# Dense layer 2 of a graph network kernel: rounding moved to GpSimd, another ScalarE order, three pairs of part buffers

## The reference, cut to what matters

```python
def _bn(h, g, b):
    mean = h.mean(0)
    var = h.var(0)
    return (h - mean) * jax.lax.rsqrt(var + EPS) * g + b
...
y = x + aggr
h = jnp.maximum(_bn(y @ W1 + b1, g1, be1), 0.0)
h = jnp.maximum(_bn(h @ W2 + b2, g2, be2), 0.0)
return y + h
```

## Time and profile before

| what | value |
|---|---|
| median of three runs | 2009.98 us |
| profiled execution, and its span | 2003.11 us, 2001.3 us |
| layer 2, from its first subtraction to its last | 626.1 to 925.7 us of the span |
| its blocks 20 to 97 | 688.1 to 925.7 us, 237.6 us |
| engines in that stretch | PE 234.2 us busy, DVE 221.0, ACT 211.4, POOL 0 |
| the 16 DMA engines from 700 to 790 us | busy share 0.98, 347 GB/s |

### The profile page before, as it was taken

How to read it: one execution, slowest core, us unless ns; L and a number is a source line. 1 busy time by engine, 2 the same in 40 slices (tenths; PEclk the granted TensorE clock), 3 DMA queues, 4 the chain that set the end, 5 groups by cost and what they waited for, 6 DMA issues and landing times. The chain is left out here.

```text
span 2001.3 us, 27312 instructions
## 1 busy us (share of the span) xinstructions
PE 1774.9 (89%) x8655; PEld 1386.4 (69%) x8655; DVE 1624.2 (81%) x2365; ACT 1304.9 (65%) x1818; POOL 1088.0 (54%) x1200
## 2 busy tenths in 40 slices
PE   4687489999998999999999989965999999999994
PEld 3465378888886776766666666644788888888883
DVE  4678556766767999997999999994888888888884
ACT  1434246565656898887788888871666666666663
POOL 7556456676786400000555555566876576765553
PEclk8889899999999999999999999986999999999997
DMA  9999999999996899983699999974565532322110
GB/s 344 366 348 394 364 359 346 335 342 331 340 244 141 241 348 348 325 299 124 245 378 390 385 410 390 390 286 126 161 168 146 145 89 92 92 83 75 58 43 29
DMA packets 187567, 506.47 MB, mean 253 GB/s; under 512 B 26355, under 2 KB 79505, under 8 KB 187168
## 3 DMA queue, kind: packets, MB, share of 16 engines
q1 hardware_dynamic: 129888, 379.91, 51.9%
q0 software_dynamic: 47136, 73.62, 16.3%
q10 hardware_dynamic: 10400, 51.20, 6.7%
HBM read 323.94 MB, written 236.25 MB: 280 GB/s over the span
## 5 line engine op out<-in xcount | busy, mean ns | idle before, releaser
L607 POOL DMA_INDIRECT scratch_y<-sums,k_target x196 | 312.7, 1595 | 159.9 <-issue 79.9
L1041 ACT ACTIVATE d_o<-d_u,d_free 128x256 f32<-128x256 f32 x392 | 203.1, 589 | 64.0 <-POOL d_free L1078 64.0
L1015 PEld LDWEIGHTS d_pN<-k_ident,d_r 128*128 128x128 f32 x1568 | 192.0, 193 | 52.1 <-issue 46.4
L1010 PE MATMUL d_pN<-d_y,d_free 128*128 128x512 f32 x392 | 191.9, 612 | 33.6 <-DVE d_u L1104 30.1
L1015 PE MATMUL d_pN<-k_ident,d_r 128*128 128x128 f32 x1568 | 192.7, 276 | 4.9 <-ACT d_r L1030 4.9
L818 ACT ACTIVATE d_part_h<-pT 128x1024 fp32r<-128x1024 f32 x98 | 100.5, 1027 | 139.5 <-PE pT L785 125.1
L882 DVE TENSOR_TENSOR d_part_l<-pT,d_part_h 128x1024 fp32r<-128x1024 f32 x98 | 119.9, 1224 | 85.0 <-ACT d_part_h L818 85.0
L1075 POOL TENSOR_TENSOR d_free<-d_free,k_minus_half 128x8 f32<-128x8 f32 (+1 forms) x100 | 163.7, 1637 | 0.2
L1104 DVE SCALAR_TENSOR_TENSOR d_u<-d_pN,d_free,k_base 128x256 f32<-128x256 f32 x392 | 160.9, 472 | 0.0
L252 POOL DMA_INDIRECT k_ring<-in_x,k_src x100 | 120.9, 1209 | 68.7 <-PE pT L280 40.3
L61 PE MATMUL pU<-d_part_h,k_w_h 128*128 128x512 f32 x296 | 125.5, 424 | 27.2 <-DVE d_part_l L882 14.2
(11 more groups left out here) (227 smaller groups left out, 5209.7 us busy)
## 6 DMA issues: line engine op xcount, KB each, us to landing
scratch_h<-d_h SPq DMA_DIRECT2D x159, 512.0 KB, 5.9
out<-d_o SPq DMA_DIRECT2D x97, 520.0 KB, 6.0
k_ring<-scratch_y SPq DMA_DIRECT2D x98, 512.0 KB, 7.7
d_y<-scratch_y SPq DMA_DIRECT2D x98, 512.0 KB, 7.8
scratch_y<-in_x ACTq DMA_DIRECT2D x25, 2000.0 KB, 20.7
d_h<-scratch_h SPq DMA_DIRECT2D x81, 512.0 KB, 7.1
k_ring<-scratch_h SPq DMA_DIRECT2D x78, 512.0 KB, 5.2
attr<-in_attr_t SPq DMA_DIRECT2D x25, 512.0 KB, 15.1
```

Source lines behind the costliest of these rows:

```text
L607: pool.indirect_dma_start(out=A["y"], out_offset=bass.IndirectOffsetOnAxis(ap=K.target[:, t:t + 1], axis=0), in_=K.sums[:, t], in_offset=N ...
L1010: pe.matmul(pN[k % 4][:, 2 * two:2 * two + 2].rearrange("p j f -> p (j f)"), twice[:], y[:, k % 4, two * 2 * F:(two + 1) * 2 * F], start=T ...
L1015: last = pe.matmul(pN[k % 4][:, j, cc * P:(cc + 1) * P], r[:, k % 4, cc, j * P:(j + 1) * P], K.ident[:], start=False, stop=j % 2 == 1 and ...
L1041: last = act.activation(o[:, k % 4, j, 0:F], u[:, k % 3, j], ACT.Identity, bias=nb[:, n, j:j + 1], scale=rs[:, n, J + j:J + j + 1])
```

## The change

1. From block 20 of layer 2 on (`POOL_FROM`), GpSimd rounds every block: 78 copies of 128x1024 from r to the high part, 26 of which were ScalarE's and 52 VectorE's. Blocks 0 to 19 keep the old turn.
2. Layer 2 has three pairs of high and low parts. The third pair (`third_h`, `third_l`) lies in a piece of `sums` behind the held blocks, tiles 64 to 71. A rounding now waits for the product of block g-3 (`wait_part`), and at block 2 for the scatters that read these tiles.
3. In a turn ScalarE does `relu(g+2)` ahead of `out(g-2)`, not behind it.

```diff
+POOL_FROM = 20
...
     def hi_on_scalar(g):
-        return g % 3 == 0
+        return g % 3 == 0 and g < NB + POOL_FROM
+
+    def hi_on_pool(g):
+        return g >= NB + POOL_FROM
...
+    def parts_of(g):
+
+        at = (g - NB) % 3 if layer2(g) else g % 2
+        return (part_h[:, at], part_l[:, at]) if at < 2 else (third_h[:], third_l[:])
+
+    def wait_part(engine, g):
+
+        if g >= NB + 3:
+            engine.wait_ge(product, g - 2)
+        elif g == NB + 2:
+            for q in range(4):
+                engine.wait_ge(halved_in[q], 16 * (HELD_SUMS + 2))
+        else:
+            engine.wait_ge(product, g - 1)
...
+        for g in range(NB, 2 * NB):
+            if hi_on_pool(g):
+                pool.wait_ge(relu_done, g - NB + 1)
+                wait_part(pool, g)
+                pool.tensor_copy(parts_of(g)[0], r[:, g % 2]).then_inc(hi2_pool, 1)
...
             if hi_on_scalar(g):
                 act.wait_ge(relu_done, g - NB + 1)
-                act.wait_ge(product, g - 1)
-                act.activation(part_h[:, g % 2], r[:, g % 2], ACT.Copy).then_inc(hi2_scalar, 1)
+                wait_part(act, g)
+                act.activation(parts_of(g)[0], r[:, g % 2], ACT.Copy).then_inc(hi2_scalar, 1)
...
             if g + 1 < 2 * NB:
                 hi2(g + 1)
+            if g + 2 < 2 * NB:
+                relu(g + 2)
             if g >= NB + 2:
                 out(g - 2)
-            if g + 2 < 2 * NB:
-                relu(g + 2)
...
             if hi_on_scalar(g):
                 dve.wait_ge(hi2_scalar, on_scalar)
+            elif hi_on_pool(g):
+                dve.wait_ge(hi2_pool, on_pool)
             else:
                 dve.wait_ge(relu_done, g - NB + 1)
-                dve.wait_ge(product, g - 1)
-                dve.tensor_copy(part_h[:, g % 2], r[:, g % 2]).then_inc(hi2_vector, 1)
-                dve.wait_ge(hi2_vector, g + 1 - NB - on_scalar)
-            dve.tensor_tensor(out=part_l[:, g % 2], in0=r[:, g % 2], in1=part_h[:, g % 2].bitcast(F32),
-                              op=ALU.subtract).then_inc(lo_done, 1)
+                wait_part(dve, g)
+                dve.tensor_copy(parts_of(g)[0], r[:, g % 2]).then_inc(hi2_vector, 1)
+                dve.wait_ge(hi2_vector, g + 1 - NB - on_scalar - on_pool)
+            high, low = parts_of(g)
+            dve.tensor_tensor(out=low, in0=r[:, g % 2], in1=high.bitcast(F32), op=ALU.subtract).then_inc(lo_done, 1)
```

More of the change, by code:

```diff
@@ L650, in dense12 @@
     early = ET * 3 // 4
-    assert HELD_SUMS * J <= early
+    assert (HELD_SUMS + 2) * J <= early
     passes = [(1, k) for k in range(NB)] + [(2, (NB - HOLD + n) % NB) for n in range(NB)]
@@ L657, in dense12 @@
     part_h, part_l, h, held, r, _ = K.shared_second
+    third_h, third_l = K.shared_parts
     pT, pH = K.pT, (K.pU, K.pS.rearrange("p j f -> p (j f)").rearrange("p (c e) -> p c e", c=C))
@@ L663, in dense12 @@
         sem("turned"), sem("relu"), sem("hi"), sem("lo"), sem("product"), sem("stats"), sem("h_done"))
-    hi2_scalar, hi2_vector = sem("hi2_scalar"), sem("hi2_vector")
+    hi2_scalar, hi2_vector, hi2_pool = sem("hi2_scalar"), sem("hi2_vector"), sem("hi2_pool")
     coef = sb("coef", [P, 2, C])
@@ L800, in multiply @@
                     last = mm3(pe, bank(g)[:, oc], (K.w0_h[:, w, ic, cols], K.w0_l[:, w, ic, cols]),
-                               (part_h[:, g % 2, ic], part_l[:, g % 2, ic]), ic == 0, ic == C - 1)
+                               (high[:, ic], low[:, ic]), ic == 0, ic == C - 1)
             last.then_inc(product, 1)
@@ L886, in parts @@
             on_scalar = sum(hi_on_scalar(n) for n in range(NB, g + 1))
+            on_pool = sum(hi_on_pool(n) for n in range(NB, g + 1))
             if hi_on_scalar(g):
                 dve.wait_ge(hi2_scalar, on_scalar)
+            elif hi_on_pool(g):
+                dve.wait_ge(hi2_pool, on_pool)
             else:
                 dve.wait_ge(relu_done, g - NB + 1)
-                dve.wait_ge(product, g - 1)
-                dve.tensor_copy(part_h[:, g % 2], r[:, g % 2]).then_inc(hi2_vector, 1)
-                dve.wait_ge(hi2_vector, g + 1 - NB - on_scalar)
-            dve.tensor_tensor(out=part_l[:, g % 2], in0=r[:, g % 2], in1=part_h[:, g % 2].bitcast(F32),
-                              op=ALU.subtract).then_inc(lo_done, 1)
+                wait_part(dve, g)
+                dve.tensor_copy(parts_of(g)[0], r[:, g % 2]).then_inc(hi2_vector, 1)
+                dve.wait_ge(hi2_vector, g + 1 - NB - on_scalar - on_pool)
+            high, low = parts_of(g)
+            dve.tensor_tensor(out=low, in0=r[:, g % 2], in1=high.bitcast(F32), op=ALU.subtract).then_inc(lo_done, 1)
         def stats(g):
@@ L1690, in same_place @@
                 return made
-            (K.sums,), K.shared_sums = same_place(
+            (K.sums,), (_, *K.shared_parts), K.shared_sums = same_place(
                 nc.sbuf_tensor, (("sums", [P, S.TC, F], F32),),
+                (("d_ahead", [P, HELD_SUMS * J * F], F32), ("d_third_h", [P, C, B], F32R), ("d_third_l", [P, C, B], F32R)),
                 (("d3_h2", [P, 4, C * B], F32), ("d3_y", [P, 4, J * F], F32), ("d3_r", [P, 4, C, B], F32),
```

## The result

The changed kernel took 1987.85 us, median of four runs (1981.26 to 1988.69), where the kernel before took 2010.08 us (2009.41 to 2012.05) beside it. The ratio is 0.9882 with a 95% interval of 0.9861 to 0.9903: 22 us faster. The forecast was 1993.6 us.

What follows compares the result with a forecast made beforehand. Layer 2 was taken to be bound by engines holding each other up, afterwards by DMA, then TensorE. Savings of 14.1 and 2.3 us, total 16.4, off the median 2009.98 gave 1993.6 us; own range 1983 to 1999, with rivals 1984 to 2036.

Steps and rivals of the forecast that it cites:

- Direction and mechanism: Layer 2: three engines could each do a block in 2.8 us but lose 0.2 us handing buffers over; faster, chance 0.62.
- the sum: Layer 2: 14.1 us saved from block 20 on and 2.3 us in blocks 2 to 19, total 16.4 us.
- ScalarE's order: Layer 2: the rectifier starts some 2.3 us sooner, the eviction goes back by up to 1.5 us, at cost 0.
- The copy: GpSimd, layer 2 from block 20: each 128x1024 copy takes 1.2 us, bounded by 0.7 and 3.25 us, and is hidden.
- Turns of copy and subtraction: Layer 2: if GpSimd's copy and VectorE's subtraction exclude each other, a block needs 2.63 us, still under 2.80.
- rival 1: Layer 2: copy and subtraction take turns and the copy is over 1.7 us; at 2.1 us, 2042 us; chance 0.20.
- DMA as the bound of blocks 20 to 80: Layer 2: loads and stores hold these blocks at 2.93 us each, 178.7 us for 61, against TensorE's 2.80.
- The sign that I had named for this: Layer 2: blocks 81 to 97 no faster than 20 to 80 would mean that DMA was not the bound.
- Sums of statistics: Layer 2, two places where VectorE sums up statistics: the third pair hides them, so their 4.5 us are gone.
- at 1.00 throughout: Changed profile: TensorE's granted clock was to stay at 1.00, with no idle time behind the sums of statistics.
- Nothing given back: Stages behind layer 2: they start when it ends, with the same work, so the whole 16.4 us saving stays.

Runs made afterwards that it cites:

- e5: The changed kernel run again, beside the kernel before on another chip: 1982.52 us against 2007.51 us, ratio 0.9865.
- e3: The changed kernel but with the old ScalarE order (eviction ahead of rectifier): layer 2 took 318.0 us, ratio 0.9960 to the kernel before.
- e6: The changed kernel, but GpSimd copies each block twice, first to a free place: 2018.02 us, ratio 1.0048 to the kernel before.
- e8: The kernel before with only the new ScalarE order, two pairs of parts and no GpSimd rounding: ratio 0.9929, layer 2 14.1 us shorter.
- e7: The changed kernel, but GpSimd writes zeros to 1536 elements ahead of each copy: 1983.15 us, ratio 0.9874 to the kernel before.

## Why the prediction was right, and where it was off

- *Direction and mechanism: right.* Three engines near 2.8 us a block held each other up, and with the change TensorE sets 2.80.
- *The number: nearer than its parts.* The forecast is 5.8 us over the measured time, but layer 2 gave 25.2 us where the sum had 16.4. The 3 us between lie in the spread of the runs; beside e5's comparison, where 25 us were saved, the sum is 8.6 us short. That the first comparison came closer is luck.
- *ScalarE's order: right, and worth more than I gave it.* I named the 2.3 us by which the rectifier moves up but gave it no term of its own. It is the main part: 14.1 us alone, and without it GpSimd and the third pair bring 5.1 us together (e3).
- *The copy: right.* 1.2 us was the estimate, 1.04 is measured, from the affine_select as nearest row; the tensor_scalar's 3.0 ns an element did not carry over.
- *Turns of copy and subtraction: left open in the sum, and they do take turns.* So rival 1's mechanism is real; only its condition (a copy of over 1.7 us) was not met. e6 meets it with two copies, 2.0 us of reading, at 3.21 us a block where the rival's formula gives 2.08 + 1.23 + 0.2 = 3.51.
- *DMA as the bound of blocks 20 to 80: wrong, the mis-sized term.* I took 2.93 us a block and TensorE's 2.80 held throughout, at 378 GB/s over 175 us and up to 419 GB/s over 5. The sign that I had named for this came: blocks 81 to 97 are no faster on TensorE than 20 to 80, and relu never waited for a load. The step that failed was to read a busy share of 0.98 as being near the limit, and so to take 354 GB/s (the 347 scaled up to share 1) and the best 5 us (377) of a stretch whose blocks, at 3.03 us each, asked for no more than 347 GB/s on average, for a ceiling. This term is 7.9 us. -16.4 - 7.9 = -24.3 us, and layer 2 gave -25.2. By subtractions, blocks 20 to 97 gave 23.5 us (14.1 + 7.9 = 22.0 in the sum) and blocks 2 to 19 gave 1.6 (2.3); the first two blocks came 3.1 us closer together and what follows the last subtraction took 3.0 us longer, since a subtraction now runs a block further ahead of TensorE, which wins nothing.
- *Sums of statistics: right.* TensorE no longer stands behind them, and its clock stays at 1.00 from 690 to 900 us. It was not at 1.00 throughout, as I had put it: the first block of layer 2 runs at a lower one (0.54 from 626 to 634 us), in the kernel before as well (0.71).
- *Nothing given back: right in the timed runs,* -22 and -25 us for 25.2 us in layer 2. The profiles themselves had 3 to 7 us more behind layer 2 than the kernel before had. As the next stage is equal to 1 us in all (396.9 us before, 397.4 and 396.8 after, from first to last `d_u`), the difference lies in the edge stage: 655.2 us in the profile of the kernel before, 661.7 and 658.8 in the two of the changed one, 658.8 to 659.4 in e6 to e8. Whether the 655.2 is only a quick execution, as its time of 6.9 us under the median suggests, is not shown.

## What to carry to other kernels

When several engines are each close to the period of a loop, follow the loop that gives one buffer back through every engine's written order: here one swap of two instructions in ScalarE's order, which put an eviction behind a rectifier, was worth 14 us, and more buffers or a fourth engine were worth 2 to 5 us without it. A busy share of the DMA engines near 1 is no proof of a limit: here it was 0.98 at 347 GB/s and 0.99 at 378, and nobody waited. Take a ceiling from a stretch in which someone waits for it.

## What the runs showed of the hardware

- GpSimd copies 128x1024 fp32 to fp32r in 1042 ns and fills 128x1536 with zeros in 1380 ns, while its tensor_scalar of 128x128 took 561 ns.
- A GpSimd instruction that reads SBUF and a VectorE subtraction with both inputs in SBUF exclude each other; the one that starts second is drawn out, in the rows above to 1.55 to 1.92 us for the copy (1.04 alone) and to 1.88 to 2.03 us for the subtraction (1.21 alone). A GpSimd fill, which reads nothing, and a subtraction run side by side (e7).
- One core's loads and stores together, in transfers of 512 KB, ran at 378 GB/s over 175 us and at up to 419 GB/s over 5 us, with nobody waiting for them.
- The same kernel differs by 2% between chips (2008 and 2043 to 2050 us). Where it was profiled on a quick and on a slow one, nearly all of that lies in the last stage: 1052.2 and 1090.2 us behind layer 2, and 323.1 and 322.6 us in it.
